# Weighing side and segment values on all four quarters of the TensorE array, with GpSimd on the softmax factors and ScalarE evicting keys twice

## What is computed

```python
def dilated_mask(seq_len):
    pos = jnp.arange(seq_len)
    seg = pos // SEGMENT_LENGTH                     # 64
    local = seg[None, :] == seg[:, None]
    diff = jnp.abs(pos[None, :] - pos[:, None])
    dil = (diff > 0) & (diff % DILATION_RATE == 0) & (diff <= DILATION_RATE * SEGMENT_LENGTH)
    allowed = local | dil                           # 4 * 64
    return jnp.where(allowed, 0.0, -jnp.inf)
q = (hidden_states @ w_q).reshape(B, S, H, Dh)      # k, v in the same way
scores = jnp.einsum('bqhd,bkhd->bhqk', q, k) * scaling + mask[None, None]
attn = jax.nn.softmax(scores, axis=-1)
out = jnp.einsum('bhqk,bkhd->bqhd', attn, v).reshape(B, S, H * Dh)
return out @ w_o
```

## Time and profile before

| what | us |
|---|---|
| median of 3 runs | 473.04 (469.19 to 474.06) |
| profiled execution, span | 468.8 |
| lowest run, 0.4 above that span | 469.19 |
| PE busy | 444.4 (95%) |
| PEld busy | 350.0 (75%) |
| DVE busy | 394.0 (84%) |
| ACT busy | 333.3 (71%) |
| POOL busy | 296.6 (63%) |

### The profile page before, as it was taken

One profiled execution on the slowest core, in us unless ns is written; L12 is line 12 of the kernel. 1 busy time (PEld: TensorE's weight loads), 2 busy tenths in 40 slices (PEclk: granted clock), 3 DMA queues, 4 the chain that ended last, 5 costly groups with the idle time before them and its releaser, 6 DMA issues.

```text
span 468.8 us, 17264 instructions
## 1 busy us (share of the span) xinstructions
PE 444.4 (95%) x6440; PEld 350.0 (75%) x6440; DVE 394.0 (84%) x1344; ACT 333.3 (71%) x975; POOL 296.6 (63%) x491
## 2 busy tenths in 40 slices
PE   7997899999999999999999999998987989999996
PEld 6685688888888888788887778887744757558775
DVE  6885798987888899889887698995899989998775
ACT  3686768868877877886786678695566579987533
POOL 4321488677666858667865588564669897674322
PEclk9999899999999999999999999999999999999999
DMA  7577852346335445344455565364000000000003
GB/s 224 183 246 209 247 142 52 73 99 133 80 74 112 76 79 105 76 85 94 98 108 124 112 124 108 75 125 91 1 1 0 0 2 1 1 0 2 1 0 91
DMA packets 136099, 40.53 MB, mean 86 GB/s; under 512 B 104977, under 2 KB 131025, under 8 KB 136017
## 3 DMA queue, kind: packets, MB, share of 16 engines
q1 hardware_dynamic: 135440, 38.38, 35.7%
q10 hardware_dynamic: 576, 1.05, 0.6%
HBM read 29.44 MB, written 9.96 MB: 84 GB/s over the span
## 4 chain that ended last, share of the span: by engine, by line
PE 59%; POOL 9%; DMA 8%; DVE 8%; ACT 7%; SPq 4%; issue 3%; ACTq 0%; POOLq 0%; DVEq 0%
PE psum L422 10%; PE psum L464 10%; PE psum L484 5%; PE psum L1186 5%; DMA w_rows_dram<-st 4%; PE psum L498 4%; PE psum L495 4%; PE psum L403 4%; PE psum L510 4%; PE psum L1181 3%; PE psum L405 3%; PE psum L404 3%; DMA st<-w_rows_dram 2%; POOL area L1827 2%; ACT pband L569 2%
## 5 line engine op out<-in xcount | busy, mean ns | idle before, releaser
L948 POOL TENSOR_SCALAR pband<-pband,fac 128x192 f32<-128x192 f32 x256 | 103.9, 424 | 80.6 <-DVE fac L771 80.4
L569 ACT ACTIVATE pband<-pband,st 128x192 f32<-128x192 f32 x256 | 113.1, 447 | 1.0 <-DVE st L719 1.0
L719 DVE CUSTOM_DVE_ANT_0 pband<-psum,band_mask 128x192 f32<-128x192 f32 x256 | 76.1, 353 | 0.1
L422 PE MATMUL psum<-keys,q_class 64*64 64x192 f32 (+2 forms) x1536 | 66.2, 274 | 0.0
L464 PEld LDWEIGHTS psum<-ident,pband 128*128 128x128 f32 x384 | 45.4, 141 | 21.4 <-issue 13.3
L422 PEld LDWEIGHTS psum<-keys,q_class 64*64 64x64 f32 x1536 | 57.6, 133 | 1.4 <-issue 1.4
L464 PE MATMUL psum<-ident,pband 128*128 128x128 f32 x384 | 53.0, 273 | 2.2 <-DVE pt L780 2.2
L569 ACT ACTIVATION_READ_ACCUMULATOR pband<-pband,st 128x1 f32 x256 | 49.3, 192 | 0.0
L938 POOL COPY q_class<-q_rows 128x512 f32<-128x512 f32 x32 | 36.5, 1142 | 19.2 <-ACT q_rows L609 19.2
L930 POOL COPY keys<-k_rows 128x512 f32<-128x512 f32 x32 | 36.1, 1130 | 14.0 <-ACT k_rows L601 7.1
L780 DVE COPY pt<-psum 128x512 f32<-128x512 f32 x64 | 43.7, 683 | 0.5
(11 more groups left out here) (213 smaller groups left out, 1090.7 us busy)
## 6 DMA issues: line engine op xcount, KB each, us to landing
v_rows_dram<-arena SPq DMA_DIRECT2D x32, 256.0 KB, 3.4
v_both<-v_rows_dram SPq DMA_DIRECT2D x32, 256.0 KB, 3.8
v_seg<-v_rows_dram SPq DMA_DIRECT2D x64, 128.0 KB, 3.6
v_side<-v_rows_dram SPq DMA_DIRECT2D x96, 64.0 KB, 2.6
w_rows_dram<-st SPq DMA_DIRECT2D x64, 8.0 KB, 3.0
st<-w_rows_dram SPq DMA_DIRECT2D x64, 8.0 KB, 2.5
arena<-_attn_hidden_states_dram SPq DMA_DIRECT2D x4, 256.0 KB, 3.7
out_dram<-x SPq DMA_DIRECT2D x4, 256.0 KB, 2.5
```

The lines of the kernel that those rows point to most:

```text
L422: return pe.matmul(bank[2 * r + head][rows, at:at + y.shape[1]], x, y, start=True, stop=True, skip_group_check=True)
L569: act.activation(x, x, ACT.Exp, bias=mine[:, head:head + 1], scale=-1.0, accum_out=mine[:, 2 + head:3 + head]).then_inc(s_exp, 1)
L719: dve.tensor_tensor_reduce(pband[:, G % P_SLOTS, c, head, :], bank[2 * r + head][:, at:at + BAND], band_mask[:, (0, 1, 1, 2)[w], SEG * (1 ...
L948: pool.tensor_scalar(x, x, fac[:, F % 2, 1, c, head:head + 1], 1.0, ALU.mult, ALU.mult).then_inc(s_scaled, 1)
```

## The change

1. `weigh_segments` takes the place of `weigh(U, 3)`: the values of a segment's 64 tokens lie on partitions 0 to 63 or 64 to 127 by the half of the window they are in, for both heads. A product's rows are then chosen by the window half and its columns by the head. Window halves are kept apart in PSUM as well: the output of the first half is in bank 6, of the second in bank 7, 256 columns each. `weigh_sides` takes the place of `weigh(U, 2)` in the same way, in two parts: first the products whose rows and bank go together as they do for the segments, and later the crossed ones, behind the semaphore `s_sides`.
2. `weigh` for b = 0 and 1 has to write the two halves apart: 16 products of 64 queries for 8 of 128.
3. The layout of probabilities (`pband`, `pseg`) and of values (`v_side`, `v_seg`) follows; the DMAs of values are as many, in pieces of 512 bytes for 256.
4. Banks: queries are projected into bank 6 and keys into bank 7, in turn with the output halves; the output product goes to bank 4 in place of bank 7. So weighing waits until queries and keys have been copied out, and a projection until the output has been.
5. ScalarE copies the keys out of bank 7 twice, in rows (`take_keys`) and in class order (`take_class_keys`); `keys_by_class` of GpSimd is gone.
6. GpSimd makes the differences, products, totals and factors of the softmax; VectorE keeps the joint minimum and the reciprocal (`joints`, `invert`).
7. The order within a step is new on every engine, and so are the lists of calls of the start, the drain and the tail.

The core of the diff:

```diff
-                if b == 2 and w < NW - 1:
-                    pe.wait_ge(s_v[w + 1], (p + 1) * V_DMAS[w + 1])
...
+                if b == 0:
+                    pe.wait_ge(s_query, min(U + FIRST_STEP, NS_ALL))
+                    pe.wait_ge(s_key, min(U + FIRST_STEP + 1, NS_ALL))
+                    pe.wait_ge(s_kclass, min(U + FIRST_STEP + 1, NS_ALL))
                     wait(pe, s_out, U)
...
+            def weigh_segments(U):
...
+                mine = turned(U, 3)
+                for j in range(2):
+                    for second in range(2):
+                        for head in range(2):
+                            for half in range(2):
+                                dims, mykeys = slice(DH * head, DH * (head + 1)), slice(SEG * half, SEG * (half + 1))
+                                cols, at = SEG * (2 * j + second), P * (2 * j + head) + SEG * second
+                                last = pe.matmul(out_bank[half][dims, cols:cols + SEG],
+                                                 v_seg[mykeys, HALF_SEGS * w + 2 * j + second, dims],
+                                                 mine[mykeys, at:at + SEG], start=False, stop=False, skip_group_check=True)
+                last.then_inc(s_pv[1], 1)
+
+            def weigh_sides(U, crossed):
...
+                if crossed:
+                    pe.wait_ge(s_sides, U + 1)
+                for d in range(2):
+                    for head in range(2):
+                        for odd in range(2):
+                            half = odd ^ crossed
...
             for t in range(FIRST_STEP, DRAIN):
-                project(t, 1)
                 weigh(t - 6, 0)
                 weigh(t - 6, 1)
-                turn(t - 6, 3)
-                output(t - 7)
+                scores(t - 2, 0)
+                weigh_segments(t - 6)
+                weigh_sides(t - 6, 0)
+                scores(t - 2, 1)
+                weigh_sides(t - 6, 1)
                 turn(t - 5, 0)
-                weigh(t - 6, 2)
-                scores(t - 2, 0)
-                weigh(t - 6, 3)
-                scores(t - 2, 1)
+                turn(t - 5, 1)
                 project(t, 0)
-                turn(t - 5, 1)
                 turn(t - 5, 2)
+                project(t + 1, 1)
+                turn(t - 5, 3)
+                output(t - 6)
...
+            def take_class_keys(t):
...
+                act.copy(keys[:, p % 2, :, PAD + P * w:PAD + P * (w + 1)],
+                         shared_bank.rearrange("p (x c) -> p c x", c=DIL)).then_inc(s_kclass, 1)
```

More of the change, by code:

```diff
@@ L477, in weigh @@
[L477 to L486 removed]
+                mine = turned(U, b)
@@ new lines, in totals @@
+            def totals(F):
+                if not there(F):
+                    return
+                pool.wait_ge(s_ediff, F + 1)
+                wait(pool, s_total, F)
+                pool.tensor_tensor(part[:, :, :, :, :], ediff[:, :, :, :, :], st[:, F % P_SLOTS, :, :, :, 2:4],
+                                   ALU.mult).then_inc(s_chain, 1)
+                pool.wait_ge(s_chain, F + 1)
+                wait(pool, s_inverse, F)
+                pool.tensor_tensor(total[:, :, :, :], part[:, 0, :, :, :], part[:, 1, :, :, :],
+                                   ALU.add).then_inc(s_total, 1)
```

463 lines of the change are left out of this document (247 added, 216 removed).

## The result

The changed kernel is slower: 486.38 us (median of 4 runs, 483.28 to 488.87) against 472.13 of the kernel before (4 runs, 469.19 to 474.06), a ratio of 1.032 with a 95% interval of 1.026 to 1.038. I had forecast 455.

The account below looks back on a forecast made before the run. TensorE's order and rate were taken to bound the loop. Gains of 13.8 (21 steps) + 0 (251 to 290) + 1 (drain) + 3.5 (start) = 18.3 us, off 473.04, gave 454.7, rounded to 455; range 446 to 468.

Parts of the forecast that it names:

- 21 steps: Main loop, TensorE-bound from 62 to 251 us: each step falls from 8.98 to 8.32 us, gaining 13.8 us.
- start: Before stage 0: TensorE's 4.04 us wait for queries and the slow clock behind it go; gain 3.5 us, bounds 0 and 5.6.
- tail: Behind 345 us: unchanged but for the order of its calls, counted at nothing, 1 us either way.
- Segments and sides: Loop products on four array quarters, 13.8 ns apart instead of 28.4: segments gain 0.47 us a step, sides 0.24.
- Sum for a step: Loop step: 8.98 - 0.47 - 0.24 + 0.04 - 0.09 = 8.22 us, if nothing new waits.
- rival 1: Loop: quarters give little, as records cannot be supplied faster; 470 us, or 465 at 25 ns a record; chance 0.13.
- The first of rival 1's two times: Loop: records supplied no faster than the pairs are now, a step of 9.03 us, total 470.
- Weighing by class: Loop: 32 records of 64 queries replace 16 of 128, 0.91 us against 0.87, costing 0.04 a step.
- 251 to 290 and the drain: After the loop: SP-bound steps gain 0 (2 lost to 3 gained); drain, 290 to 345 us, gains 1 (0 to 3).
- Rival 2: ScalarE's key copy by class as dear as GpSimd's 1.14 us: a step of 8.72, total 463; chance 0.15.
- Rival 3: Loop: statistics return late to VectorE in each step; slower, 485 us, or 477 if half the steps; chance 0.08.
- these handovers: Loop: waits on ScalarE's copies of keys and output from shared banks, bounds 0 and about 0.3 us, taken as 0.1.

## Why the prediction was wrong

The terms of the sum, as gains in us on the profiled span:

| term | forecast | measured |
|---|---|---|
| 21 steps | 13.8 | -0.6 |
| from stage 21 to the last output product | 1 | 2.6 |
| start | 3.5 | -0.8 |
| tail | 0 | -14.0 |
| sum | 18.3 | -12.8 |

Two terms failed, the steps by 14.4 and the tail by 14.0.

**Segments and sides: the size was right, the worth was not.** 13.9 ns per record, and 8.33 us for a step less its holes against 8.32, are as forecast. The first step that failed is "Sum for a step", where I wrote that it holds "if nothing new waits", and took no account of the supply of instructions: the holes took 12.3 of the 13.8 us forecast, and two waits in step 0 another 1.4. I weighed a slower supply (rival 1) as a pace of each record, and looked for it in the distance of two starts. It comes as holes instead, at 16 of the 32 places in these steps where a 256th instruction falls. The first of rival 1's two times has the loop right by its result (9.03 a step; measured 9.00), but by luck: the records do start 14 ns apart.

**Weighing by class** was counted by its rate, 0.04. That it doubles the instructions of this part, from 16 records to 32, was not counted at all, and they are 32 of the 35 more in a step.

**Start: 3.5 forecast, -0.75 measured.** I had named what is late next, the first transposition behind the same statistics, and the lower bound, 0; I chose a value near the middle of the range. The statistics themselves came 3 us later. ScalarE's exponentials of stage 0 are not the reason, for they end at 33.1 us (33.6 before), and the run that moved them ahead sent later still. SP's queue reached the send at 38.2 (before: 36.0) and then waited 1.0 us for VectorE's sums of the segments. In VectorE's new list these stand behind the first segment maxima of stage 1 and start at 38.47, where they started at 31.91. Why SP itself came 2 us later was not tested. Step 0 waits in addition 0.84 us for VectorE's copy and 0.60 for the output weights, because output(0) was moved one step forward and the load was not; loading them earlier took that wait away, and step 0 still took 10.05.

**251 to 290 and the drain** gave 2.6 us up to the last output product, where I had 0 and 1, in spite of holes there too (2.3 us from start to start at 256.48).

**The tail at nothing (1 us either way)** is the second step that failed, by 14.0 us. I read "not changed but for the order of its calls" as no change. 8 to 10 of it are the order of the body, shown in both directions. The other 5 to 6 (7.4 by the trace of the run with the old body) arise behind the last output product, where PE has waits that before has not. They are put down to the new order between that product and the third group, shown on the kernel before only.

**Rivals.** Rival 2 is out: the copy by class takes 0.60 us on ScalarE, where the copy in rows takes 0.59. Rival 3 is out: VectorE waited for statistics 3 times in the 21 steps, 2.3 us in all. Only this rival led to the slower side, and I gave that side 0.08; the slower end came from places that I had priced at zero. The rows of ScalarE are the answer to the earlier trace rows. PE's lines in the loop name no wait for a copy of ScalarE's. The 0.1 a step that I took for these handovers is about what lies between 8.33 and 8.22, but no row shows that it is they.

```profile
205.38 0.59 ACT L661 COPY k_rows<-psum 128x512 f32<-128x512 f32 x1 [0.42 <-PE psum L420]
205.86 0.60 ACT L669 COPY keys<-psum 128x512 f32<-128x512 f32 x1
```

## What to carry to other kernels

Where many small instructions stand in one run, count them, and not only their time. From the start of a packet until PE goes on it takes 2.2 to 2.7 us here, while PE uses up some 90 small instructions in one; a rate gained by finer tiles can be lost in the same loop, as here, if the instructions come in one run. An order of calls in in-order queues is a change like any other: give the stretch whose calls are reordered a price of its own, and both signs, and look for waits that an earlier stage's new use of a bank puts into it.

## What the runs showed of the hardware

- PE's instructions are fetched while the program runs, in packets of 16 KB, 256 instructions of 64 bytes (56 packets on q8). A hole on PE, from start to start, lasted up to 2.3 us (at 256.48 in the changed kernel) and ended 1.2 to 1.6 us after the packet. With 64 instructions put ahead, the holes moved by 64.
- A change of tile shape between 64x64 and 128x128 cost 0.14 us each: two more of them per step added 0.28 (8.25 to 8.53).
- Records of 64 columns on four quarters start 13.9 ns apart over 32 in a row.
- In the tail, PE waited 2.9 us up to 426.37, and its granted clock was 0.50 from 427 to 430 and 0.79 over 418 to 434; with the calls in the old order the clock over 418 to 434 was 1.00.
